# Three 16-head attentions rebuilt on transposed scores in PSUM

## The chip, the cores and the metric

One core of a Trainium2 chip runs the whole network as one launch. The metric is device microseconds of that launch, the median of several runs; lower is better. TensorE (PE), VectorE (DVE), ScalarE (ACT), GpSimd (POOL) and the DMA queue of SyncE (SP) run side by side and meet only at semaphores.

## What is computed

The reference is four layers of gated cross-attention and feed-forward over x of shape 128 x 64 x 128 (8192 tokens, float32), with a context of the same shape:

```python
x = x + tanh(g_xattn[l]) * attention_l(layernorm(x), ctx, ctx)
x = x + tanh(g_ffn[l])   * ffn_l(layernorm(x))
```

Layer 0 has heads of 64 columns and a routed expert feed-forward. Layers 1, 2 and 3 have 16 heads of 8 columns each; these three attentions are what is changed. For each batch of 64 tokens and each head:

```python
score = q_h @ k_h.T / sqrt(8)            # 64 x 64
# layer 1: softmax   layer 2: score where mask else -1e9, then softmax
# layer 3: s = where(score >= 0, score + 1, 1 / (1 - score)); s / sum(s)
out   = p @ v_h
```

Layer 1's feed-forward is a quantised one (bitlinear), those of layers 2 and 3 are routed to 8 experts, top-2 and top-1.

## The kernel before, in words

`build` (L2312) calls the stages one after another, with a barrier of all engines between them. `attention_narrow` (L522) is called three times: "l1" (softmax, with a head), "l2" (masked, with a tail), "l3" (stable, with both). Head (L176) fetches each token's expert row by indirect DMAs on POOL and adds it to x before the attention. Tail (L233) normalises the new x, multiplies it with the router's weights, picks experts and scatters rows to `slots` by indirect DMAs.

Each attention is a software pipeline over 32 items of 256 tokens (4 batches of 64). All engines have the same order written out by hand: `step(t)` emits the piece of each item that is due in beat t, and `t.live(s)` is true where item t-s exists. So a beat holds scores of one item, transposes of the one before, outputs of the one before that, and a semaphore count orders each piece against the others.

In a beat PE makes the scores of an item (L873, 16 matmuls that each use 32 rows and 64 columns of the array), projects q and k (L892, L893), transposes the probabilities 16 times through the two banks PT (L903), projects the values (L925), multiplies them with the transposed probabilities (L979, 32 matmuls with 18 columns moving: two heads at once), and projects out (L938, or L957 in the masked kind). An fp32 matmul appears as two instructions in the trace, a transpose and a bf16 matmul as one.

The keys are masked: k_t holds four copies of the projected k, copy j with all but the 8 rows of head j of each group of 32 rows set to zero (L814, four ACT instructions from PSUM). A matmul over 32 rows then gives four heads side by side in its 256 columns.

DVE takes the row maximum of the 128 x 2048 scores from PSUM (L739), subtracts it into the SBUF tile `prob` (L742), and in the masked kind first applies the mask (L730). ACT takes the exponential in SBUF (L843). ACT then copies every transposed block out of PT (L822). In the stable kind ACT makes relu(-s) (L800), log and exp of it (L835, L838), DVE makes max(s, 0) (L721) and adds the two (L781). DVE divides by the sums, which come out of L979 as two extra columns (L703, L707).

The tail's router multiplies on POOL (L358, two of 128 x 1024 a beat; the last items on DVE, L459) and DVE sums up (L464). Choices and slots of 4 items are made in one beat by a chain of small DVE instructions (L471 to L489, L436 to L451). L328 scatters.

Of the kernel before, what the change touches and what calls it, by code (L numbers as in the profile page):

```python
# [6 lines left out]
P = 128  # L7
# [32 lines left out]
C_COLS = C_ITEM + TOP2_TILES  # L40


def constants():

    c = np.zeros((P, C_COLS), np.float32)
    c[:, C_IDENT:C_IDENT + P] = np.eye(P)
    c[:, C_TRI:C_TRI + P] = np.triu(np.ones((P, P)))
    c[:, C_ONES:C_ONES + P] = 1.0
    for j in range(4):
        c[:, C_JMASK + j] = (np.arange(P) % 32) // 8 == j  # L50
    c[:, C_ECOL:C_ECOL + EXPERTS] = np.arange(EXPERTS)
    c[:, C_BLK:C_BLK + 16] = np.arange(16) * SLOTS
    c[:, C_ITEM:] = np.arange(TOP2_TILES)
    return c
# [121 lines left out]
class Head:  # L176
# [5 lines left out]
    def __init__(self, ph, g, rows, ks, own):  # L182
        self.g, self.rows, self.ks, self.own = g, rows, ks, own
        self.index = ph.sb("index", [P, 2, ks, 2], U32)
        self.got = ph.sb("got", [P, 2, ks, 2, D])
        self.term = ph.sb("term", [P, ks + own, 2, D])
        self.arrived = [ph.sem(f"arrived{k}") for k in range(2)]
        self.index_done, self.terms_done, self.combined = ph.sems("index_done terms_done combined")
        self.partly = [ph.sem(f"partly{k}") for k in range(ks + own - 1)]

    def gather(self, nc, pool, t, s, ready, count):

        g, n0, n2 = self.g, t.done(s), t.done(s + 2)
        pool.wait_ge(ready, count)
        for k in range(self.ks):
            last = nc.gpsimd.tensor_copy(self.index[:, t.par(s), k, :], g.get[k][:, bass.ds(t.item(s) * 2, 2)])  # L196
        last.then_inc(self.index_done, 1)
        for k in range(self.ks):
            for tile in range(2):
                pool.wait_ge(ready, count)  # L200
                wait(pool, self.index_done, n0)
                wait(pool, self.terms_done, n2)
                pool.indirect_dma_start(self.got[:, t.par(s), k, tile, :], None, self.rows,  # L203
                                        bass.IndirectOffsetOnAxis(ap=self.index[:, t.par(s), k, tile:tile + 1], axis=0),
                                        bounds_check=self.rows.shape[0] - 1, oob_is_err=False).then_inc(self.arrived[t.par(s)], 16)

    def combine(self, nc, pool, t, s, ready, count):

        g, n1, n2 = self.g, t.done(s), t.done(s + 1)
        landed = t.landed(s, 2 * self.ks)  # L210
        tiles = bass.ds(t.item(s) * 2, 2)
        xs = g.x[:, tiles, :]
        pool.wait_ge(ready, count)
        wait(pool, self.arrived[t.par(s)], landed)

        wait(pool, self.combined, n2)
        for k in range(self.ks):
            last = nc.gpsimd.tensor_tensor(self.term[:, k, :, :], self.got[:, t.par(s), k, :, :],
                                           g.weight[k][:, tiles].unsqueeze(2).broadcast_to([P, 2, D]), ALU.mult)
        if self.own:  # L220
            last = nc.gpsimd.tensor_tensor(self.term[:, 1, :, :], g.xn[:, tiles, :],
                                           g.weight[1][:, tiles].unsqueeze(2).broadcast_to([P, 2, D]), ALU.mult)
        last.then_inc(self.terms_done, 1)
        pool.wait_ge(ready, count)
        wait(pool, self.terms_done, n1)
        nc.gpsimd.tensor_tensor(self.term[:, 0, :, :], self.term[:, 0, :, :], self.term[:, 1, :, :],
                                ALU.add).then_inc(self.partly[0], 1)
        pool.wait_ge(ready, count)
        wait(pool, self.partly[0], n1)
        nc.gpsimd.tensor_tensor(xs, xs, self.term[:, 0, :, :], ALU.add).then_inc(self.combined, 1)  # L230


class Tail:  # L233

    def __init__(self, ph, g, w, bias, kind, slots, tiles):
        self.g, self.w, self.bias, self.kind, self.slots, self.tiles = g, w, bias, kind, slots, tiles
        self.ks = 2 if kind == "top2" else 1
        self.nb = BATCH_TILES // tiles
        wide, narrow = [P, BATCH_TILES, EXPERTS], [P, BATCH_TILES]
        self.w_s, self.bias_s = ph.sb("router_w", [P, EXPERTS, D]), ph.sb("router_b", [P, EXPERTS])
        self.st, self.mv = ph.sb("tail_st", [P, 2, tiles, 6]), ph.sb("tail_mv", [P, 2, tiles, 2])
        self.var_eps, self.rstd = ph.sb("tail_var_eps", [P, 2, tiles]), ph.sb("tail_rstd", [P, 2, tiles])  # L250
        self.prod = ph.sb("products", [P, tiles, EXPERTS, D])
# [9 lines left out]
        self.put = ph.sb("put", [P, 2, self.ks, tiles], U32)  # L261
        self.rows = ph.sb("rows_out", [P, 2, tiles, D])
        (self.w_in, self.part, self.stats, self.eps, self.rstd_done, self.xn_done, self.multiplied, self.summed,
         self.chosen_done, self.counted, self.counts_read, self.put_done, self.rows_copied, self.chained, self.totalled) = ph.sems(
            "router_w_in tail_part tail_stats tail_eps tail_rstd_done tail_xn_done multiplied summed "
            "chosen_done counted counts_read put_done rows_copied chained totalled")
        self.sent = [ph.sem(f"sent{k}") for k in range(2)]
        self.slots_clear = None
        self.loads = 16 * (1 + (bias is not None))

        self.ph, self.steps = ph, {}

    def load(self, sp):
        sp.dma_start(self.w_s[:, :, :], self.w.partition_broadcast(P)).then_inc(self.w_in, 16)
# [18 lines left out]
    def on_dve(self, t, s):  # L293

        return t.i is None and t.item(s) >= t.items - 7

    def depth(self):

        return 5 + self.nb + 3
# [2110 lines left out]
```

## Time and profile before

| what | us |
|---|---|
| median of 3 runs | 3622.13 (3612.05 to 3623.86) |
| the profiled execution, its own time | 3616.34 |
| its span, from first to last instruction | 3614.6 |
| busy: PE / DVE / ACT / POOL | 2554.5 / 2132.0 / 1498.5 / 1596.1 |

Busy shares are 71%, 59%, 41% and 44% of the span. No single engine is busy throughout: the stages have different limits, so the profile must be read stage by stage. The page's chain of waits covers only the last piece of the run. In the rows further down, "x" counts instructions, "PEclk" is the granted TensorE clock as a part of 2.4 GHz, and an arrow names what ended an idle time.

### The profile page before, as it was taken

How to read it: one execution, taken by the hardware profiler on the slowest of the kernel's cores; microseconds unless marked ns; L12 is line 12 of the kernel's file. 1: busy time of each engine (PE TensorE's matmuls, PEld its weight loads, DVE VectorE, ACT ScalarE, POOL GpSimd, SP SyncE). 2: the span in 40 equal slices, each digit the busy share in tenths (PEclk: the TensorE clock that was granted, in tenths of full speed). 3: DMA queues.
4: the chain of work that ended last, by engine and by line, in shares of the span. 5: the costliest groups of instructions: out<-in, count | busy, mean ns of one | idle time of the engine just before them, and what ended most of it. 6: DMA issues, size and time to landing. Idle time of an engine off the chain costs nothing. (4 is left out here: it accounts for less than half of the span.)

```text
span 3614.6 us, 84054 instructions
## 1 busy us (share of the span) xinstructions
PE 2554.5 (71%) x30961; PEld 1981.4 (55%) x30971; DVE 2132.0 (59%) x4394; ACT 1498.5 (41%) x2492; POOL 1596.1 (44%) x2184
## 2 busy tenths in 40 slices
PE   5999999977678886233687766609956877665490
PEld 4878778764557775122465555506634665554260
DVE  3767777661166664676578788854424666677312
ACT  3555555532255553677343333202215665553120
POOL 1333433440164430775024666440017788884207
PEclk9999999988888887555688778659976766675795
DMA  4000000003300000000000000015531000000243
GB/s 143 17 18 22 23 21 21 20 8 112 99 26 22 22 19 13 1 1 1 26 10 12 23 22 23 20 61 153 161 106 32 23 25 27 27 23 13 79 128 93
DMA packets 192979, 153.50 MB, mean 42 GB/s; under 512 B 24426, under 2 KB 170461, under 8 KB 192582
## 3 DMA queue, kind: packets, MB, share of 16 engines
q1 hardware_dynamic: 176198, 116.45, 11.0%
q0 software_dynamic: 16384, 31.69, 2.9%
q8 instruction: 257, 4.21, 0.5%
q14 instruction: 140, 1.15, 0.1%
HBM read 97.54 MB, written 52.43 MB: 41 GB/s over the span
## 5 line engine op out<-in xcount | busy, mean ns | idle before, releaser
L979 PE MATMUL l_B<-l_val,l_prob_t 128*64 128x18 f32 x6144 | 348.6, 220 | 44.1 <-ACT l_prob_t L822 36.9
L979 PEld LDWEIGHTS l_B<-l_val,l_prob_t 128*64 128x64 f32 x6144 | 340.4, 149 | 59.3 <-issue 59.3
L903 PE MATMUL l_PT<-const_table,l_prob 128*128 128x128 f32 x1536 | 267.9, 332 | 38.0 <-ACT l_prob_t L822 28.6
L1971 PE MATMUL experts_H<-experts_xs_t,experts_w 128*128 128x512 f32 x576 | 272.1, 616 | 10.1 <-ACT experts_hid L1951 4.9
L903 PEld LDWEIGHTS l_PT<-const_table,l_prob 128*128 128x128 f32 x1536 | 237.3, 178 | 68.8 <-issue 58.0
L822 ACT COPY l_prob_t<-l_PT 128x512 f32<-128x512 f32 x384 | 209.6, 601 | 132.8 <-PE l_PT L903 132.7
L203 POOL DMA_INDIRECT l_got<-rows,l_index x192 | 220.2, 1147 | 94.7 <-POOL l_index L196 50.3
L358 POOL TENSOR_TENSOR l_products<-l_router_w,xn_all 128x1024 f32<-128x1024 f32 x100 | 236.3, 2390 | 32.3 <-DVE logits L464 32.0
L883 PE MATMUL l_A<-const_table,l_xn 128*128 128x128 f32 x192 | 59.6, 410 | 251.7 <-issue 139.1
L328 POOL DMA_INDIRECT slots<-xn_all,put x192 | 202.0, 1052 | 60.6 <-issue 49.5
L632 POOL TENSOR_TENSOR l_var_eps<-l_mv,eps 128x2 f32<-128x2 f32 x96 | 26.4, 275 | 430.4 <-DVE l_mv L775 430.3
L196 POOL COPY l_index<-get 128x2 uint32<-128x2 uint32 x96 | 15.4, 177 | 435.2 <-DVE l_recip L659 435.2
L1372 POOL TENSOR_TENSOR l_var_eps<-l_mv,eps 128x1 f32<-128x1 f32 x64 | 12.1, 189 | 438.4 <-DVE l_mv L1454 438.4
L1990 PE MATMUL experts_Y<-experts_w,experts_hid 128*128 128x128 f32 x1664 | 198.8, 276 | 4.1 <-DVE experts_hid L1931 2.2
L1990 PEld LDWEIGHTS experts_Y<-experts_w,experts_hid 128*128 128x128 f32 x1664 | 192.6, 193 | 6.0 <-issue 6.0
L883 PEld LDWEIGHTS l_A<-const_table,l_xn 128*128 128x128 f32 x192 | 25.9, 190 | 308.1 <-issue 308.1
L807 ACT COPY l_xn_t<-l_A 128x256 f32<-128x256 f32 x96 | 35.6, 370 | 371.9 <-PE l_A L883 371.9
L814 ACT ACTIVATE l_k_t<-l_B,l_bk_masked,const_table 128x256 f32<-128x256 f32 x384 | 184.9, 568 | 0.0
L1411 DVE TENSOR_REDUCE l_top<-l_S 128x16 f32<-128x1024 f32 x64 | 78.3, 1224 | 172.0 <-PE l_S L1561 172.0
L1971 PEld LDWEIGHTS experts_H<-experts_xs_t,experts_w 128*128 128x128 f32 x576 | 104.5, 197 | 126.9 <-issue 126.9
L843 ACT ACTIVATE l_prob<-l_prob 128x2048 f32<-128x2048 f32 x64 | 122.9, 1921 | 117.9 <-DVE l_prob L742 117.9
L1907 DVE COPY experts_xs_t<-experts_X 128x512 f32<-128x512 f32 x72 | 49.8, 692 | 205.0 <-PE experts_X L1979 205.0
(309 smaller groups left out, 6835.8 us busy)
## 6 DMA issues: line engine op xcount, KB each, us to landing
experts_w<-in_F_w SPq DMA_DIRECT2D x104, 256.0 KB, 2.9
experts_xs<-slots SPq DMA_DIRECT2D x72, 256.0 KB, 2.8
rows<-experts_y SPq DMA_DIRECT2D x72, 256.0 KB, 2.9
l_ctx_t<-in_ctx_t SPq DMA_DIRECT2D x96, 128.0 KB, 2.1
slots<-l_zeros SPq DMA_DIRECT2D x64, 96.0 KB
experts_w<-in_F_w SPq DMA_DIRECT2D x40, 128.0 KB, 2.5
slots<-l_zeros SPq DMA_DIRECT2D x8, 512.0 KB, 5.5
l_ctx_t<-in_ctx_t SPq DMA_DIRECT2D x64, 64.0 KB, 2.0
```

What stands on the lines that cost most here:

```text
L203: pool.indirect_dma_start(self.got[:, t.par(s), k, tile, :], None, self.rows, bass.IndirectOffsetOnAxis(ap=self.index[:, t.par(s), k, tile ...
L328: pool.indirect_dma_start(self.slots, bass.IndirectOffsetOnAxis(ap=g.put[c][:, tile:tile + 1], axis=0), g.xn[:, tile, :], None, bounds_che ...
L358: last = nc.gpsimd.tensor_tensor(self.prod[:, tile, :, :], self.w_s[:, :, :], g.xn[:, bass.ds(t.item(s + 2) * k + tile, 1), :].broadcast_t ...
L814: last = nc.scalar.activation(k_t[:, t.par(3), j, :], B[:, 256:512], ACT.Identity, bias=bk_masked[:, j:j + 1], scale=g.const[:, C_JMASK + ...
L822: nc.scalar.copy(prob_t[:, 4 * c:4 * c + 4, :], PT[:, c % 2, :].rearrange("p (a q) -> p a q", a=4)).then_inc(pt_drained[c], 1)
L843: nc.scalar.activation(flat, flat, ACT.Exp).then_inc(prob_ready, 1)
L883: last = nc.tensor.transpose(A[:, P * tile:P * tile + P], xn[:, t.par(2), tile, :], ident)
L903: last = nc.tensor.transpose(PT[:, c % 2, P * a:P * a + P], prob[:, t.par(5), c, a // 2, 2 * (a % 2):2 * (a % 2) + 2, :].rearrange("p j k ...
L979: last = nc.tensor.matmul(B[64 * b:64 * b + 64, col:col + 18], prob_t[:, 4 * (hp // 2) + 2 * tile + hp % 2, 64 * b:64 * b + 64], val[:, t. ...
L1411: nc.vector.tensor_reduce(top[:, :, :], S[:, :, :, :], AX.X, ALU.max).then_inc(top_done, 1)
L1971: nc.tensor.matmul(H[:, c, :], w1_s[:, t.par(2), c, :], xs_t[:, t.par(2), :], start=True, stop=True).then_inc(h_filled[c], 1)
L1990: last = nc.tensor.matmul(Y[:, P * k:P * k + P], hid[:, t.par(3), c, P * k:P * k + P], w2_s[:, t.par(3), c, :], start=c == 0, stop=c == FC ...
```

## The change

`attention_narrow` becomes `attention_split` for all three layers, and `Tail` and `Router` (the class that layer 0 used) become one `Router`.

- Scores are computed twice in the softmax and masked kinds. SCORE fills the four banks X with the scores (queries in partitions); DVE reduces the maximum from them and they are dropped. The maximum is split into three bf16 parts, transposed by one matmul (TOP), spread with a mask of its own on DVE (top_d), and in the next beat PROB fills the four banks Z with "minus maximum" (16 bf16 matmuls) plus the transposed scores (keys in partitions). ACT takes exp straight from Z. The stable kind has no maximum and makes only the transposed scores.
- With keys in partitions the probabilities need no transposes. OUT multiplies them with the values in 64 matmuls of 64 rows x 64 columns, 9 columns moving, that go round the four quarters of the array. In the stable kind the two terms are not added: each is a matmul of its own, 128 in all, the two of a pair in the same quarter one behind the other.
- ACT writes q, four masked copies of q, k and four masked copies of k (ten instructions from PSUM; five in the stable kind).
- The mask is added by bf16 matmuls with the identity: 8 of 256 columns into X and 8 into Z.
- ACT copies the values; the bias of values and of the output projection is a bf16 matmul over 3 rows.
- The router's scores are PE work: two transposes, an ACT copy, two matmuls. Indices and rows of the indirect DMAs are read in place instead of copied first on POOL.
- Banks are shared: X by SCORE, TOP, output projection, router; Z by PROB, q/k (bank 0), values (bank 1), OUT (banks 2 and 3). The stable kind has q/k in X.

PE's order in a beat, cut to its core:

```diff
+                if t.live(PROB):
+                    wait(pe, qk_drained, t.done(PROB))
+                    if stable:
+                        wait(pe, plus_done, 4 * t.done(PROB + 1))
+                    else:
+                        wait(pe, diag_done, t.done(PROB))
+                        wait(pe, qk_drained, t.done(PROJ + 1))
+                    wait(pe, xv_drained, beats(t.t - 1, TURN, XV_BEATS))
+                    wait(pe, o_drained, t.done(OUT + 1))
...
+                                    nc.tensor.matmul(Z[64 * b:64 * b + 64, r, 256 * tile:256 * tile + 256], minus_ones[rows, :],
+                                                     top_d[rows, t.par(PROB), 4 * tile:4 * tile + 4, 64 * b:64 * b + 64],
...
+                                last = nc.tensor.matmul(Z[64 * b:64 * b + 64, r, 256 * tile:256 * tile + 256], k_t[rows, slot, seq],
+                                                        q_m[rows, slot, :, seq], start=stable and tile == 0, stop=tile == 1 and not folded)
...
+                    last.then_inc(p_filled, 1)
+                if t.live(SCORE) and not stable:
...
+                    last.then_inc(s_filled, 1)
+                if t.live(PROJ):
...
+                    if not stable:
+                        bank_read(t, 0)
...
+                if stable:
+                    stream_out(t)
+                if t.live(TURN) or t.live(PROB):
...
+                    bank_read(t, 1)
...
+                if t.live(OUT):
+                    wait(pe, prob_done, t.done(OUT) if stable else 4 * t.done(OUT))
+                    if stable:
+                        wait(pe, plus_done, 4 * t.done(OUT))
...
+                    bank_read(t, 2)
+                    bank_read(t, 3)
...
+                    for h in range(16):
+                        for tile in range(2):
+                            for b in range(2):
+                                rows, side = slice(64 * b, 64 * b + 64), 64 * (b ^ tile)
+                                for k, term in enumerate(terms):
...
+                if not stable:
+                    stream_out(t)
+                if t.live(SCORE) and not stable:
+                    wait(pe, split_done, t.done(SCORE))
+                    nc.tensor.matmul(TOP, split[:, :, :, :].rearrange("p r s a -> p (r s a)"), g.const_bf[:, C_IDENT:C_IDENT + P],
...
+                if turns(t):
...
+                if ranks(t):
```

ACT's order in a beat: the four exponentials (or relus), the q and k copies, the copies of xn and values, then the copy of the turned blocks (`wait(act, turned_filled, ...)`), and in the stable kind log and exp last. DVE's: maximum and its three parts, reciprocal and division of OUT, top_d, add to x, normalise, statistics, router. POOL's: rstd, combine, gather, scatter. In the masked kind POOL first makes one of the two expanded masks:

```diff
+                nc.gpsimd.tensor_scalar(hide[:, 1, :, :], mask_raw[:, 1, :, :], HIDE, -HIDE, ALU.mult, ALU.add).then_inc(hidden, 1)
```

## Rows read from the trace of the kernel before

**Rows 1.** Busy time by stage: layer 0, and the stretches of l1, l2, l3

```profile
core 0: us, PE busy (x) PEld busy (x) DVE busy (x) ACT busy (x) POOL busy (x), PEclk, DMA share, GB/s
0.00:968.60 968.60, 856.71 (x14344) 693.18 (x14344) 565.09 (x1300) 439.06 (x707) 300.18 (x452) 0.97 0.16 46
968.60:1427.60 459.00, 366.52 (x4544) 296.26 (x4544) 253.06 (x455) 219.33 (x385) 185.33 (x288) 0.81 0.08 21
...
1725.50:2411.50 686.00, 439.78 (x5001) 343.45 (x5001) 515.70 (x965) 213.53 (x353) 332.87 (x306) 0.75 0.06 22
...
2680.30:3383.30 703.00, 439.53 (x4616) 346.53 (x4616) 429.35 (x844) 340.82 (x449) 519.51 (x562) 0.64 0.09 26
```

**Rows 2.** Instructions on the scores tile: ns min/median/max, start of first and last

```profile
L730 DVE TENSOR_TENSOR l_prob<-l_S,l_limit x64: 1214/1216/1226, 1751.2 to 2305.0; 128x1024 f32<-128x1024 f32 x64
L739 DVE TENSOR_REDUCE l_top<-l_S x32: 2260/2292/2294, 1007.9 to 1394.4; 128x32 f32<-128x2048 f32 x32
L800 ACT ACTIVATE l_soft<-l_S x32: 1877/1877/1878, 2731.8 to 3292.1; 128x2048 f32<-128x2048 f32 x32
```

**Rows 3.** Waits in 1100:1300, 1900:2290, 2850:3250: us in total, times, longest

```profile
DVE l_recip L703 <- PE l_B L979: 53.5, 15, 4.2
...
ACT l_prob L843 <- DVE l_prob L742: 84.3, 20, 5.1
...
ACT l_soft L800 <- DVE l_prob L781: 110.2, 21, 9.4
```

**Rows 4.** Groups by line over the whole run: busy us, mean ns of one

```profile
L903 PE MATMUL l_PT<-const_table,l_prob 128*128 128x128 f32 x1536 | 267.9, 332 | 38.0 <-ACT l_prob_t L822 28.6 <-issue 8.3 <-DVE l_prob L781 0.6
...
L358 POOL TENSOR_TENSOR l_products<-l_router_w,xn_all 128x1024 f32<-128x1024 f32 x100 | 236.3, 2390 | 32.3 <-DVE logits L464 32.0
...
L822 ACT COPY l_prob_t<-l_PT 128x512 f32<-128x512 f32 x384 | 209.6, 601 | 132.8 <-PE l_PT L903 132.7
...
L814 ACT ACTIVATE l_k_t<-l_B,l_bk_masked,const_table 128x256 f32<-128x256 f32 x384 | 184.9, 568 | 0.0
...
L742 DVE TENSOR_TENSOR l_prob<-l_prob,l_top 128x2048 f32<-128x2048 f32 x32 | 90.9, 2841 | 3.3
```

**Rows 5.** Timeline, PE's bursts: start us, length us, instructions

```profile
401.50 1.16 PE L1576 MATMUL l_O<-l_prob_t,l_val 64*64 64x64 f32 x64
...
1203.68 0.67 PE L892 MATMUL l_B<-l_xn_t,l_wq 128*128 128x256 f32 x2
...
1207.98 0.71 PE L938 MATMUL l_B<-l_wo,l_ctx_out_t 128*128 128x128 f32 x4
...
1702.17 1.01 PE L2291 MATMUL bit_HT<-const_bf,bit_hq 128*128 128x128 bf16 x8 [3.77 <-DVE bit_hq L2195]
...
1749.07 2.02 PE L873 MATMUL l_S<-l_k_t,l_q_t 32*64 32x256 f32 x32 [2.54 <-ACT l_k_t L814]
...
2004.80 1.12 PE L873 MATMUL l_S<-l_k_t,l_q_t 32*64 32x256 f32 x32
...
2016.73 1.09 PE L957 MATMUL l_A<-l_wo,l_ctx_out 128*64 128x128 f32 x8
...
2019.19 2.92 PE L979 MATMUL l_B<-l_val,l_prob_t 128*64 128x18 f32 x58
```

**Rows 6.** Timeline, small steps of DVE and POOL and the end of l2

```profile
1202.37 0.36 DVE L703 RECIPROCAL l_recip<-l_B 128x32 f32<-128x32 f32 x1 [3.32 <-PE l_B L979]
...
1202.83 0.49 DVE L707 TENSOR_TENSOR l_ctx_out<-l_B,l_recip 128x128 f32<-128x128 f32 x2
...
2345.30 0.26 DVE L471 TENSOR_REDUCE l_of_batch<-l_chosen 128x8 f32<-128x64 bf16 x1
...
2349.44 0.23 DVE L489 TENSOR_TENSOR l_chosen<-l_hot 128x64 bf16<-128x64 f32 x1
...
2405.23 0.97 POOL L328 DMA_INDIRECT slots<-xn_all,put  x1 [0.30 <-issue]
2406.51 0.97 POOL L328 DMA_INDIRECT slots<-xn_all,put  x1 [0.30 <-issue]
```

More of the change, by code:

```diff
@@ L210, in combine @@
-        landed = t.landed(s, 2 * self.ks)
-        tiles = bass.ds(t.item(s) * 2, 2)
+        g, par, n = self.g, t.par(s), t.done(s)
+        tiles = slice(t.item(s) * 2, t.item(s) * 2 + 2)
         xs = g.x[:, tiles, :]
+        others = (self.got[:, par, 0, :, :], g.xn[:, tiles, :] if self.own else self.got[:, par, 1, :, :])
         pool.wait_ge(ready, count)
[L214 to L219, printed above, removed]
@@ L400, in dve, with transpose @@
-    def dve(self, nc, dve, t, s, updated):
+        return nc.tensor.matmul(bank[:, 0:n], ones, self.before[:, :].unsqueeze(1).broadcast_to([P, BATCH_TILES, EXPERTS]),
+                         start=False, stop=True)
+    def transpose(self, nc, pe, t, s, out):
+        wait(pe, self.xn_done, t.done(s + 2))
+        for tile in range(self.tiles):
+            last = nc.tensor.transpose(out[:, P * tile:P * tile + P], self.g.xn[:, t.item(s + 2) * self.tiles + tile, :], self.g.const[:, C_IDENT:C_IDENT + P])
+        return last
@@ new lines, in score, with read_transposed, read_scores @@
+    def score(self, nc, pe, t, s, out):
+        for tile in range(self.tiles):
+            last = nc.tensor.matmul(out[:, EXPERTS * tile:EXPERTS * tile + EXPERTS], self.xn_t[:, t.par(s + 3), tile, :], self.w_s[:, :],
+                                    start=True, stop=True)
+        return last
+    def read_transposed(self, nc, t, s, bank):
+        return nc.vector.tensor_copy(self.xn_t[:, t.par(s + 2), :, :], bank[:, 0:P * self.tiles].rearrange("p (k n) -> p k n", n=P))
+    def read_scores(self, nc, t, s, bank):
+        k = self.tiles
+        return nc.vector.tensor_copy(self.g.logits[:, bass.ds(t.item(s + 3) * k, k), :],
+                                     bank[:, 0:EXPERTS * k].rearrange("p (k e) -> p k e", e=EXPERTS))
@@ L519, in chain, with beats, attention_split @@
         return link
-def attention_narrow(nc, g, name, gate_col, wq, bq, wk, bk, wv, bv, wo, bo, kind, mask=None, head=None, tail=None):
-    ITEMS, TPI = TILES // 2, 2
+def beats(t, first, n):
+    return max(0, min(t - first + 1, n))
+def attention_split(nc, g, name, gate_col, wq, bq, wk, bk, wv, bv, wo, bo, kind, mask=None, head=None, router=None):
+    ITEMS = TILES // 2
     SCALE = float(1.0 / np.sqrt(np.float32(8)))
-    folded = kind == "masked"
+    HIDE = float(2.0 ** 100)
+    folded, stable = kind == "masked", kind == "stable"
+    STAT, NORM, TURN, PROJ = 1, 2, 3, 4
+    SCORE, PROB, OUT, STREAM = 5, 6, 7, 8
+    SLOTS_QK, SLOTS_CTX = 4, 8
+    LAST = STREAM + 1
     with ExitStack() as ctx:
@@ L578, in _, with turns, ranks, reused @@
+        TURNED_BEATS = (ITEMS + (T0 + 2 if tail else OUT)) - TURNED_FROM
+        RANKS_BEATS = ITEMS + 1
+        def turns(t):
+            return (not folded and t.live(OUT)) or (tail and t.live(T0 + 2))
+        def ranks(t):
+            return tail and (t.live(T0 + 3) or tail.batch(t, T0 + 4))
+        def reused(t, s, slots):
+            return 16 * ((t.t - s) // slots + 1) if t.t >= s else 0
         @block.sync
@@ new lines, in step @@
+                    if folded:
+                        pe.wait_ge(hidden, 2)
+                        for tile in range(2):
+                            for r in range(4):
+                                last = nc.tensor.matmul(Z[:, r, 256 * tile:256 * tile + 256], g.const_bf[:, C_IDENT:C_IDENT + P],
+                                                        hide[:, 1, 2 * t.item(PROB) + tile, :].unsqueeze(1).broadcast_to([P, 4, 64]),
+                                                        start=False, stop=tile == 1)
```

1063 lines of the change are left out of this document (395 added, 668 removed).

## The prediction

> **What bounds the kernel now.** I cut the run into stages first, since only three of them change. l1, l2 and l3 take 459, 686 and 703 us, 1848 of 3614.6; the rest stays [rows 1]. Then I took the beat of each: 31 steps between the first and the last score instruction give (1394.4 - 1007.9)/31 = 12.5 us for l1, (2303.9 - 1751.2)/31 = 17.8 for l2 (the last L730 is the second of its beat, 1.1 us in), (3292.1 - 2731.8)/31 = 18.1 for l3 [rows 2]. The remainder of a stage is its start and end. Last, the waits of the steady middle tell who is late. In l1 DVE waits for PE's output matmuls in every beat and PE is busy 80% of the stage: PE bounds it. In l2 ACT waits for DVE's subtraction and DVE has 515.7 busy us of 686: DVE bounds it. In l3 ACT waits for DVE's add up to 9.4 us, while POOL is busy 519.5 of 703: a ring over DVE, PE and ACT with POOL close behind [rows 1, 3].
>
> **What goes.** Of PE: 16 transposes a beat, 1536 in all, 332 ns each with overlap, 267.9 us busy. Of ACT: their four copies at 601 ns. Of DVE: the subtraction (2.3 to 2.8 us a beat in l1 and l2), the two masks at 1.2 us (l2), the add (l3), and the router's sum (l2, l3). Of POOL: the router's products, 2.39 us twice a beat [rows 2, 4].
>
> **What comes, priced at full clock, one beat.** Sixteen score matmuls are 1.1 us, against 2.0 at the low clock, and a q/k projection is 2 x 0.6 us [rows 5]. The 16 "minus maximum" matmuls stream as many columns in one bf16 pass, not four: 0.3 us. Eight mask matmuls: the 128-column bf16 ones took 1.01/8 = 126 ns each in a stage at the low clock, so 256 columns at twice the clock are again 126 ns, 1.0 us for eight. Transposes of xn, value bias and values: 0.4 + 0.1 + 0.7 = 1.2. Output projection: 8 instructions in 1.1 us plus bias is 1.2, twice that in l2 [rows 5]. A bank of 512 columns read by ACT is about 0.6 us, a masked copy of 256 columns just under 0.5 in a run of four (568 ns with overlap) [rows 4]. The maximum stays 2.3 us; its three parts are four dependent small DVE steps at 0.3 (15 such steps run from 2345.30 to 2349.67) [rows 2, 6]; top_d reads PSUM like L730, 1.2 us [rows 2].
>
> The unknown is OUT: 128 instructions (l1, l2) or 256 (l3) on quarters of the array. No row has this shape. The nearest below is L1576, also 64 x 64 and going round the quarters: 64 in 1.16 us, 18 ns each. The nearest above is L979, which stays in one half for 16 instructions: 58 in 2.92 us, 50 ns [rows 5]. I take 18, since shape and rotation are L1576's: 2.3 us, and 4.6 in l3.
>
> **l1.** The ring is PE and DVE: PROB 1.4, SCORE to 2.5, q/k to 3.7, values to 4.9 (ACT's exponentials end at 1.4 + 0.2 + 2.1 = 3.7 and hold up nothing), OUT to 7.2, projection to 8.4, TOP to 8.5, top_d with its two handovers to 10.0, and the next PROB waits for that. ACT beside it: 3.7 + 10 copies (4.8) + two copies (0.8) = 9.3, so the masked copies are covered by 0.7 us, no more. PE idles 1.5 us of 10. Before it was idle about as little and got a clock of 0.81 [rows 1]. I add 0.5: **10.5**. Gain 31 x 2.0 = 61.
>
> **l2.** With the masks PROB is 2.4 and SCORE ends at 4.5; q/k 5.7, values 6.9, OUT 9.2, projection 11.6, TOP and top_d 13.1. DVE has about 11.1 of work in a plain beat: 2.3 + 1.2 + 0.9 [rows 6] + 1.2, and some 5.5 for stream, two normalisations with statistics, and a quarter of the choices and slots. The choices (4.4 us in one beat of four) make DVE late for the next maximum by some 4 us, of which PE's own work hides 2: 0.7 us a beat. With the clock **14.5**. Gain 31 x 3.3 = 103.
>
> **l3.** ACT holds the ring: from the first relu, four relus and DVE's last maximum 3.1, OUT to 7.7, division and handovers (0.36 + 0.49 + 0.2) to 8.8, four transposes to 9.7, ACT's copies to 10.6, log and exp (2.0 + 1.9) to 14.6, because the next relu stands behind them. The q and k copies lie under OUT. POOL is under it: 519.5/32 = 16.2 busy us a beat now, less 4.8 for the products, is 11.5 [rows 1, 4]. PE has a hole of some 3 us while it waits for the next relus, so part of OUT runs at the low clock as in the stage before (0.64): + 2, **16.5**. Gain 31 x 1.6 = 49.
>
> **Starts and ends.** Each start has a chain of seven small DVE steps for the biases, +2 to +3. In l2 POOL expands 4096 mask bytes before its first root. DVE's mask pass before was 2.3 us; POOL's products run at 2.39 us per 1024, four times that is 9.6 [rows 4]. I take 8, near POOL's own row, and 2 for the second mask load. From the last L730 to the end of l2 it was 2411.5 - 2305.0 = 106 [rows 1, 2]. Without the router's products on DVE I count 41 until the last item is normalised, then POOL's 36 scatters at 1.28 apart [rows 6], 46, and 4 to the next stage: 91, 15 less. l3 has half the scatters, 18 or 23, but its last choices and slots are late by 4: 91 becomes 33 + 27 + 11 = 71, 20 less. Sum: l1 +3, l2 -3, l3 -17. Layer 0 loses a POOL copy that nothing waits for; its POOL is busy 300 of 969 us [rows 1]: 0. ctx loads run 8 slots ahead instead of 2; PE waited for none before: 0.
>
> **Sum.** -61 - 103 - 49 + 3 - 3 - 17 = -230. From the profiled time of 3616.3 that is 3386; this execution lay 6 below the median, so **3390**.
>
> **A rule that speaks against it.** L979 stays on all 128 rows and costs 50 ns an instruction, L1576 changes its rows at every matmul and costs 18 [rows 5]. The Trainium skill, "TensorE: Matmul & The Clock Gate", Part 3, says that a weight load overlaps running matmuls only when its row group differs. By that rule the pairs of l3, two matmuls on the same 64 rows, would lose part of the overlap, and the sum is that of the first rival; the trace agrees with it in both rows, though neither has pairs.
>
> **Rivals.**
> - *l3's pairs don't overlap.* Half of the 256 instructions at 50 ns and half at 18 is 8.7 us, 4.1 over the forecast, all on l3's ring: beat 20.6, 31 x 4.1 = 127, **3517**. For: pairs are adjacent. Against: PE may run ahead across quarters. Chance 0.17.
> - *The clock stays low in the new holes.* If l3 runs at the low clock throughout, OUT doubles (+4.6) and transposes (+0.8): 20 instead of 16.5, +108; if l1 and l2 get 0.7 instead of about 0.9, +1.5 each a beat, +93. One of the two gives about **3490**. For: l3 had 0.64. Against: PE's load rises in l1 and l2. Chance 0.15.
> - *Slower.* The quarters don't overlap at all. Then OUT costs 50 ns for 512 instructions over the three layers, 32 x 0.512 x 31 = 508 us more, **3898**. Each ns per instruction costs 15.9 us, so the loss begins at 18 + 230/15.9 = 32 ns. What decides it is whether PE works on quarters side by side when each matmul streams 9 columns only and the weight loads are all there is. For: L979. Against: L1576 with the same weight loads. A milder form at 36 ns gives 3676. Chance 0.08.
> - *It doesn't do what it says.* The "DMAs between buffers on chip" are in neither kernel here, so that part of the title is worth 0; the rest is in the code. Inside the forecast.
>
> **Numbers.** Forecast 0.60, rivals 0.17, 0.15, 0.08. Low end: full clock everywhere and late choices hidden, 0.5, 1.0 and 1.9 us a beat less, -105 and rounding for a quicker OUT: 3280. High end: the first rival: 3520. Faster 0.91, within 0.3% (some 11 us, about what a measurement of this kernel can tell from no change) 0.02, slower 0.07.
>
> **What would show it.** Score instructions of l1, l2, l3 10.5, 14.5 and 16.5 us apart; OUT as bursts of 2.3 and 4.6 us; PE waiting for top_d at most 1.5 us a beat in l1; ACT never idle between OUT's copies and the next relu in l3; POOL's mask pass of 8 us at the start of l2; the clock of l1 and l2 at 0.85 or more. The forecast is wrong if OUT costs over 25 ns an instruction, if ACT's ten copies end later than top_d, or if l3's beat is over 18.

## The result, and the profile after

The changed kernel takes **3364.9 us** (median of 4 runs, 3360.4 to 3368.2) where the kernel before takes 3618.3 beside it: a ratio of 0.930, 95% interval 0.928 to 0.932. The profiled execution spans 3358.6 us against 3614.6, so 256 us went. The kernel before takes the same in every session below (3617 to 3626); the changed one does not, and run again unchanged in one later session it took 3656.

By stage (the new kernel's windows: us, then busy time of PE, PEld, DVE, ACT, POOL with instructions, the granted clock, DMA share, GB/s; the first three are l1, l2 and l3, the others their steady middles):

```profile
967.00:1358.00 391.00, 308.36 (x7392) 223.40 (x7392) 219.74 (x527) 237.86 (x545) 179.82 (x256) 0.76 0.09 25
1655.30:2198.00 542.70, 413.23 (x8392) 319.32 (x8393) 299.44 (x958) 240.33 (x545) 185.90 (x257) 0.84 0.09 28
2464.90:3126.70 661.80, 489.54 (x10184) 391.64 (x10184) 225.01 (x835) 295.30 (x481) 335.45 (x448) 0.57 0.10 27
1010.00:1330.00 320.00, 277.25 (x6836) 202.32 (x6844) 199.14 (x466) 221.88 (x509) 154.04 (x220) 0.81 0.09 24
1690.00:2090.00 400.00, 359.19 (x7560) 276.36 (x7560) 249.58 (x765) 224.20 (x508) 118.15 (x180) 0.93 0.07 22
2520.00:3020.00 500.00, 422.07 (x8900) 336.21 (x8900) 185.16 (x662) 259.46 (x421) 266.62 (x364) 0.59 0.10 28
```

Against [rows 1], l1 lost 68 us, l2 143 and l3 41; the rest of the kernel lost 4. DVE fell from 515.7 to 299.4 us in l2 and POOL from 519.5 to 335.5 in l3, as the removals say. The beats, as one instruction's 32 places in l1, l2 and l3:

```profile
L717 DVE TENSOR_TENSOR l_top_d<-l_X,const_table x32: 1212/1224/1225, 1009.3 to 1336.7; 128x1024 bf16<-128x1024 f32 x32
L717 DVE TENSOR_TENSOR l_top_d<-l_X,const_table x32: 1216/1225/1226, 1693.4 to 2108.0; 128x1024 bf16<-128x1024 f32 x32
L701 DVE RECIPROCAL l_recip<-l_Z x32: 356/358/358, 2544.3 to 3080.0; 128x32 f32<-128x32 f32 x32
```

(1336.7 - 1009.3)/31 = 10.6, (2108.0 - 1693.4)/31 = 13.4, (3080.0 - 2544.3)/31 = 17.3 us. Forecast were 10.5, 14.5 and 16.5.

**l1.** One seam between two beats (start, duration, engine, idle time before it and who ended it):

```profile
1103.90 0.49 DVE L709 TENSOR_TENSOR l_ctx_out<-l_Z,l_recip 128x128 f32<-128x128 f32 x2
1104.40 1.22 DVE L717 TENSOR_TENSOR l_top_d<-l_X,const_table 128x1024 bf16<-128x1024 f32 x1
1104.82 0.45 ACT L797 COPY l_val<-l_Z 128x256 f32<-128x256 f32 x1
1105.83 0.83 PE L852 MATMUL l_Z<-l_top_d,l_minus_ones 32*64 32x256 bf16 x16 [0.88 <-DVE l_top_d L717]
```

TensorE waits for top_d, which ends at 1105.62; ScalarE's tenth masked copy and its values copy are done at 1105.27, only 0.35 us earlier. The steps are the forecast's.

**l2.** TensorE's order in a plain beat, which wraps round from 1880.62 of the next one:

```profile
1873.59 0.71 PE L920 MATMUL l_Z<-l_wv,l_ctx_t 128*128 128x128 f32 x4
1874.23 2.21 PE L940 MATMUL l_Z<-l_val,l_prob_t 64*64 64x9 f32 x128
1876.37 0.29 PE L989 MATMUL l_X<-l_bias_rows,const_bf 3*64 3x256 bf16 x1
1878.86 0.23 PE L950 MATMUL l_X<-const_bf,l_split 128*128 128x128 bf16 x1
1880.62 0.42 PE L852 MATMUL l_Z<-l_top_d,l_minus_ones 32*64 32x256 bf16 x16 [0.95 <-issue]
1880.83 1.07 PE L860 MATMUL l_Z<-l_q_m,l_k_t 32*64 32x256 f32 x32
1881.84 1.05 PE L866 MATMUL l_Z<-l_hide,const_bf 128*128 128x256 bf16 x8
1882.72 1.04 PE L884 MATMUL l_X<-l_hide,const_bf 128*128 128x256 bf16 x8
1883.69 1.12 PE L892 MATMUL l_X<-l_k_m,l_q_t 32*64 32x256 f32 x32
```

The prices stand: masks 1.0 us for eight, scores 1.1, OUT 2.2 (17 ns an instruction). Neighbours overlap by 0.1 to 0.2 us at each seam, so a plain beat is 12.5 us and not 13.1. The clock was 0.93 in the steady middle: 1.00 in the plain beats, 0.75 to 0.88 in those of 13.9 us and more.

**l3.** From one division to the next relus, and the next OUT's end:

```profile
2750.31 0.36 DVE L701 RECIPROCAL l_recip<-l_Z 128x32 f32<-128x32 f32 x1 [6.97 <-PE l_Z L940]
2751.39 0.66 PE L960 MATMUL l_X<-const_table,l_ctx_out 128*128 128x128 f32 x2 [1.19 <-DVE l_ctx_out L709]
2752.57 0.37 ACT L804 COPY l_ctx_out_t<-l_X 128x256 f32<-128x256 f32 x1 [7.62 <-PE l_X L348]
2753.10 2.02 ACT L812 ACTIVATE l_soft<-l_soft,const_table 128x2048 f32<-128x2048 f32 x1
2755.21 1.91 ACT L815 ACTIVATE l_soft<-l_soft 128x2048 f32<-128x2048 f32 x1
2757.03 2.04 ACT L772 ACTIVATE l_soft<-l_Z 128x512 f32<-128x512 f32 x4
2757.69 2.49 DVE L695 TENSOR_SCALAR l_prob_t<-l_Z 128x512 f32<-128x512 f32 x4 [1.16 <-issue]
2767.45 0.36 DVE L701 RECIPROCAL l_recip<-l_Z 128x32 f32<-128x32 f32 x1 [7.27 <-PE l_Z L940]
```

ScalarE goes from the copies through log and exp to the relus without a gap, as forecast, and idles 7.6 us beside OUT. OUT runs from 2760.4 to 2767.3, 6.9 us for 256 instructions, nearly all of it at the low clock (0.56 in this burst, 0.50 in most).

**Start of l2.** POOL's mask pass took 3.6 us, not 8:

```profile
1665.63 3.64 POOL L597 TENSOR_SCALAR l_hide<-l_mask_raw 128x4096 bf16<-128x4096 uint8 x1 [19.15 <-DMA l_mask_raw<-in_mask]
1665.71 3.56 DVE L634 SCALAR_TENSOR_TENSOR l_bq_masked<-const_table,l_bq 128x4 f32<-128x4 f32 x1
1674.59 0.48 DVE L734 BATCH_NORM_STATS2 l_st<-x_stream 128x6 f32<-128x128 f32 x2
```

### The profile page after: what moved, and what is told of

The parts are those of the page before. It is cut to its first block and busy times, and to the rows that moved or that the text cites. A ratio compares the mean times of both kernels' runs of the same rounds, so it can differ in the third digit from the quotient of the medians.

```text
span 3358.6 us, 107440 instructions
## 1 busy us (share of the span) xinstructions
PE 2519.9 (75%) x42779; PEld 1927.9 (57%) x42779; DVE 1673.6 (50%) x4452; ACT 1498.1 (45%) x2876; POOL 1241.9 (37%) x1925
## 5 line engine op out<-in xcount | busy, mean ns | idle before, releaser
L200 POOL DMA_INDIRECT l_got<-rows,get x192 | 197.8, 1030 | 486.1 <-DVE l_bias_rows L651 436.8
L940 PE MATMUL l_Z<-l_val,l_prob_t 64*64 64x9 f32 x12288 | 352.1, 218 | 8.5 <-issue 6.0
L940 PEld LDWEIGHTS l_Z<-l_val,l_prob_t 64*64 64x64 f32 x12288 | 338.8, 160 | 23.4 <-issue 16.1
L940 PE MATMUL l_Z<-l_val,l_soft 64*64 64x9 f32 x4096 | 216.2, 247 | 2.7 <-issue 2.3
L774 ACT ACTIVATE l_prob_t<-l_Z 128x512 f32<-128x512 f32 x256 | 132.2, 602 | 189.4 <-PE l_Z L866 89.8
L674 DVE TENSOR_REDUCE l_top<-l_X 128x32 f32<-128x2048 f32 x64 | 146.6, 2290 | 133.3 <-PE l_X L892 133.3
L940 PEld LDWEIGHTS l_Z<-l_val,l_soft 64*64 64x64 f32 x4096 | 210.3, 214 | 3.7 <-issue 3.6
L860 PE MATMUL l_Z<-l_q_m,l_k_t 32*64 32x256 f32 x3072 | 160.9, 546 | 1.5 <-ACT l_val L797 0.9
L1685 ACT ACTIVATE experts_hid<-experts_H,experts_b_scaled 128x512 f32<-128x512 f32 x128 | 78.2, 689 | 158.5 <-DVE experts_b_scaled L1645 155.3
L1254 PE MATMUL l_R<-l_ctx_t,l_wk 128*128 128x128 f32 x1024 | 132.5, 283 | 0.0
```

The source lines that it names most:

```text
L674: V.tensor_reduce(top[:, :, :].rearrange("p r a -> p (r a)"), X[:, :, :].rearrange("p r (a k) -> p (r a) k", k=64), AX.X, ALU.max).then_in ...
L774: nc.scalar.activation(prob_t[:, t.par(PROB), r, :], Z[:, r, :], ACT.Exp).then_inc(prob_done, 1)
L860: last = nc.tensor.matmul(Z[64 * b:64 * b + 64, r, 256 * tile:256 * tile + 256], k_t[rows, slot, seq], q_m[rows, slot, :, seq], start=stab ...
L940: last = nc.tensor.matmul(Z[side:side + 64, 2 + b, 9 * h:9 * h + 9], term[rows, t.par(OUT), h // 4, col:col + 64], val[rows, t.par(OUT), t ...
L1254: last = nc.tensor.matmul(R[:, BANK[name], P * k:P * k + P], w[:, 4 * (c % 2) + k, :], moving, start=True, stop=True)
L1685: nc.scalar.activation(hid[:, t.par(2), c, :], H[:, c, :], ACT.Gelu if kind == "gelu" else ACT.Relu, bias=b1_scaled[:, t.par(2), c:c + 1], ...
```

## The experiments

After the first there were five sessions on four chips, called A to E here (D and E on one chip); the kernel before took 3621, 3618, 3621, 3626 and 3617 us in them. Times are medians, or the one time there is (experiments 2, 3, 4, 5 and 9). The changed kernel doesn't take the same in all sessions, so a comparison across two of them is named as one. The diffs are cut, and a comment in them stands for code in words.

**Session A. 1: ScalarE's log and exp before the turned copies.**

```diff
+    if t.live(PROB) and stable:      # log and exp, moved up
+        ...
     if turns(t):
         act.wait_ge(ready, 1)
         ...
-    if t.live(PROB) and stable:
-        ...
```

> The new kernel with ScalarE's log and exp of the third attention issued before the copies of the turned output instead of behind them; nothing else is changed. Theory: ScalarE holds l3's ring, as predicted, and its 2.0 + 1.9 us stand in it while ScalarE idles 7.9 us beside OUT. Then the beat of 17.3 us loses 4.1 and goes to 13.2, unless TensorE at the low clock (some 15.3 us of work a beat) comes first: between 13.2 and 15.3, 62 to 127 us less, 3240 to 3303. Rival 1, TensorE is already the bound of l3 at its low clock: at most the hole of 1.2 us before the transposes goes, beat about 16.5, 3340. Rival 2, GpSimd bounds (11.5 us): it would show at a beat below 13 only.

**2 and 3: the order of OUT.** Loops were h, tile, b. Now:

```diff
-for h in range(16):
-    for tile in range(2):
-        for b in range(2):
+for b in range(2):                   # 2: same rows, output side alternates
+    for h in range(16):
+        for tile in range(2):
...
+for b in range(2):                   # 3: same quarter
+    for tile in range(2):
+        for h in range(16):
```

> OUT's loops are turned so that 32 instructions in a row (64 in l3) have their weights in the same 64 rows, alternating only the half of the output partitions; same instructions, same sums. Theory, the row group decides what overlaps: an instruction costs 50 ns as L979 did and not 17, OUT takes 6.4 us in l1 and l2 (+4.2 a beat, all on PE's path) and 12.8 in l3 (+5.9): 32 x 14.3 = 458 us more, 3820. Rival, the side of the output is enough to keep two loads going, or the weight load alone is the price: OUT stays at 2.2 and 6.9 us, 3365.

> As the run before, but each quarter of the array does its 16 (32 in l3) instructions in a row, so neither rows nor output side alternate. If the row group decides, the time is that of the run before (3820 if 50 ns an instruction). If a change of the output side was what saved the run before, this one alone is slow: 3820 against 3365. If nothing of the order matters, both are 3365.

**4: pairs apart in l3.**

```diff
 for h in range(16):
+    for k, term in enumerate(terms):
         for tile in range(2):
             for b in range(2):
-                for k, term in enumerate(terms):
```

> In l3 the two instructions of a pair (same 64 rows, same output) are no longer adjacent: the order goes round the four quarters with the positive part, then round them with the other. l1 and l2 are unchanged. Theory: pairs cost nothing, and OUT takes 6.9 us in l3 for the low clock alone (27 ns an instruction at a granted clock of 0.56): OUT stays within 0.3 us of 6.9 and the time within 10 us of 3365. Rival, the first rival of the prediction in a smaller size: adjacent pairs lose their overlap and are what lifts 4.6 to 6.9; then OUT falls by up to 2.3 us, 32 x 2.3 = 74, to 3291.

Measured: 3623.5 us (ratio 1.000, 0.999 to 1.002), 3950.7, 4588.7 and 3652.2. The first and the last made no sense: 258 and 287 us more for edits that touch l3 alone. The beats of l1 had grown too, to 13 us, and OUT's line showed why ("who waited for it" of OUT, in us and times; the new kernel's first run, then experiment 1):

```profile
  DVE l_recip L701: 304.0, 88
```

```profile
  DVE l_recip L701: 528.2, 90
```

VectorE waits 224 us longer for OUT's end, most of the 258. TensorE stands still inside OUT for nothing that the profile shows, which it calls "issue": 28.0 us in 65 waits in the first run and 292.6 in 665 here. That count takes in the matmuls and their weight loads side by side, so it tells of the same stall twice; on the matmuls alone it is 8.3 and 128.5 us, and short stalls are not in it. It serves as a marker, not as a sum. Where no such waits fall, the order's effect is plain. One burst of OUT in l1, for the new kernel, experiment 2 and experiment 3, and the two halves of the last one (us, busy time of PE and PEld with instructions, clock, DMA share, GB/s):

```profile
1111.79 2.21 PE L940 MATMUL l_Z<-l_val,l_prob_t 64*64 64x9 f32 x128
```

```profile
1431.61 3.70 PE L940 MATMUL l_Z<-l_val,l_prob_t 64*64 64x9 f32 x128
```

```profile
1103.41 8.95 PE L940 MATMUL l_Z<-l_val,l_prob_t 64*64 64x9 f32 x128
```

```profile
1103.41:1107.90 4.49, 4.49 (x84) 4.49 (x85) 1.00 0.21 58
1108.00:1112.30 4.30, 4.30 (x46) 4.27 (x44) 0.50 0.01 4
```

The first two bursts are at full clock. The third is so only in its first half, where an instruction takes 54 ns (4.49 us for 84); the whole burst's 70 ns is a mean over both clocks. So at full clock it is 17 ns an instruction when it goes round four quarters, 29 when the rows stay and the output side alternates, 54 when one quarter does all: about 1 to 2 to 4, once the last matmul's own time is taken off (15, 28, 54). Both theories for 2 missed: 29 lies between 17 and 50. Experiment 3 has the 50 ns that its first theory named, but took 4589 us and not 3820, since much of it ran at the low clock. One thing was not separated: OUT writes each of the two row halves to a PSUM bank of its own, so experiment 2 stops the alternation of rows and of banks together; the step from 2 to 3 changes the output side alone.

Experiment 4's OUT takes 6.8 us in the last beats of l3, where no such waits fall, as the new kernel's does.

**Session B. Control.** Nothing is edited.

> The new kernel again, unchanged, as a control. In the four runs before this one TensorE stalls inside OUT in l1 too, where the first and the last of them leave its instructions as they are: in gaps of about 0.65 us after every eighth instruction, 'issue' idle time of 293 us before the OUT instructions against 28 in the first run of the new kernel. The gaps stop at the beat at which the context loads run out (l1 and l3, beat 25 of 32), so they hang on transfers that run beside OUT. Theory, the supply of TensorE's instructions varies with the placement of a run, not with the edits: the control too takes up to 260 us more than 3365. Rival, the edits (ScalarE's order, the order of OUT) cause it in some way: the control is at 3365 within 10, and its OUT takes 1.8 us in l1 and 6.8 in l3.

Measured: 3364.6 us, ratio 0.930 (0.926 to 0.934), "issue" 25.0 us in 53 waits. That is the number the rival named. The edits were still possible as the cause, so the control went along with them.

**Session C. Control, experiment 1 again, and 5: top_d early.**

```diff
-V.tensor_tensor(top_d[...], ...).then_inc(diag_done, 1)
+for half in range(2):
+    V.tensor_tensor(top_d[:, ..., 4*half:4*half+4, :], ...).then_inc(diag_done, 1)
...
+# PE: per tile, wait for that half, then 'minus maximum', then scores
...
+# l2: TOP between the two halves (b) of the output projection
```

> The new kernel unchanged, a second control, on the same chip as the two runs after it. Theory 1, the supply of TensorE's instructions hangs on the chip: OUT takes the same in all runs of one chip, either 1.8 us in l1 in all of them or over 3 us in all. Theory 2, it hangs on the program: the control has 1.8 us and 3365 again wherever it runs.

> ScalarE's log and exp before the copies of the turned output, the same kernel as in the first run, beside the control on its chip. Theory 1 (the chip decides): with an undisturbed supply it gives what was expected then, a beat of 13.2 to 15.3 in l3 and 3240 to 3303 in all; if the control is slow on this chip too, it is slow by the same 258. Theory 2 (the program decides): 3620 again, with OUT at 3.5 us in l1, although TensorE's instructions are the same, one by one, as in the control.

> Two parts in l1 and l2. In both, top_d is made in two halves and TensorE starts on the first ('minus maximum' and scores of the first tile) while VectorE makes the second. In l2 alone the turning of the maximum (TOP) stands in the middle of the output projection and not behind it. Theory, TensorE's wait for top_d sets l1's beat: its hole of 0.9 us shrinks by 0.6, and the clock falls less: l1's beat 10.56 goes to 9.5 to 9.9, 20 to 33 us less. In l2 a hole of some 0.9 us goes too and the late maximum of the choices is hidden: 13.4 to 12.2 to 12.8, 19 to 37 less. Together 3295 to 3325 where the control is at 3365. Rival, ScalarE's masked copies, only 0.35 us earlier than top_d, come last as soon as top_d is early: l1 gains at most 0.35 x 31 = 11 us.

Measured: control 3655.6 (ratio 1.008, 1.006 to 1.011), experiment 1 3617.4 (0.998, 0.996 to 1.000), experiment 5 3638.5. The unchanged kernel is 290 us slower here than in B, and by 0.8% slower than the kernel before. So it is the place or the time of the run, and not the program; the kernel before doesn't show it. Beside this control experiment 1 gains 38 us and experiment 5 (one run) 17. In the beats that no stall falls on, the edits show what they are worth: experiment 1's last beats of l3 take 15.5 against 17.3, experiment 5's early beats of l2 mostly 11.0 to 11.7 against 12.5, its late ones of l1 10.2 against 10.3. What stands beside the waits? One burst of OUT in l1 of this control in its four pieces, with GpSimd's issues, and then the issues beside the first run's burst:

```profile
1119.82 1.09 POOL L200 DMA_INDIRECT l_got<-rows,get  x1 [0.16 <-issue]
1119.93 0.87 PE L940 MATMUL l_Z<-l_val,l_prob_t 64*64 64x9 f32 x44
1121.09 0.32 PE L940 MATMUL l_Z<-l_val,l_prob_t 64*64 64x9 f32 x5 [0.30 <-issue]
1121.21 1.00 POOL L200 DMA_INDIRECT l_got<-rows,get  x1 [0.31 <-issue]
1121.86 0.24 PE L940 MATMUL l_Z<-l_val,l_prob_t 64*64 64x9 f32 x2 [0.45 <-issue]
1122.60 1.36 PE L940 MATMUL l_Z<-l_val,l_prob_t 64*64 64x9 f32 x77 [0.50 <-issue]
```

```profile
1111.54 1.09 POOL L200 DMA_INDIRECT l_got<-rows,get  x1 [0.16 <-issue]
1112.93 1.00 POOL L200 DMA_INDIRECT l_got<-rows,get  x1 [0.30 <-issue]
```

While GpSimd issues a gather, TensorE gets its instructions a few at a time, 0.7 to 0.8 us apart, and when the gathers are through, 77 come in one go. In the first run the same gathers lie beside the burst of 2.21 us above, without a stall. Over the three layers an OUT instruction of this control took 58 to 72 ns while GpSimd was issuing and 24 to 29 otherwise, by where one draws the borders of an issue (the next expectation's 3859 in 241 us is 62 and not 58); in the first run it took 21 to 22 in both. In l1 the stalls end at beat 25, where the gathers do; in l2 they begin after eleven beats, with the scatters. The loads of the context are not the cause: in l2 they run from the first beat on, and the first eleven bursts take 1.8 to 2.3 us as in the first run. OUT's bursts together are 571 us long here and 347 in the first run, 224 of the 291 us; the rest lies outside OUT. The profile has a second sign of such a session. VectorE and ScalarE have waits in it that it puts down to no instruction of this core, "remote"; this control's longest group, and one of experiment 6 of the next session (us, times, longest):

```profile
DVE l_top L674 <- remote: 32.5, 5, 7.7
```

```profile
ACT l_soft L775 <- remote: 37.9, 17, 2.7
```

Every run of sessions A and C has such waits, and neither the first run nor the one of B has any.

**Session D. 6: GpSimd's gathers and scatters wait for OUT, and 7: all early issues.**

```diff
+if t.live(OUT):
+    pool.wait_ge(ready, 1)
+    wait(pool, o_filled, t.done(OUT))
 if head and t.live(0):
     head.gather(nc, pool, t, 0, ready, 1)
```

Experiment 7 is 1 and 5 together, and in l3 the router's product goes ahead of the turned transposes:

```diff
+if stable:
+    rank(t)                          # the block 'if ranks(t)', as a function
 if turns(t):
     ...
-if ranks(t):
-    ...
+if not stable:
+    rank(t)
```

> The new kernel with one wait more: GpSimd issues the gathers and scatters of a beat only when OUT of that beat has ended (before it issued them when its own queue came to them, in part beside OUT). Reason: in the runs at 3617 to 3656, an OUT instruction took 58 ns (3859 of them in 241 us) while GpSimd was issuing an indirect DMA and 25 to 27 ns otherwise, against 20 to 25 in both cases in the runs at 3365. Theory, the issue of indirect DMAs keeps TensorE's instructions away on some chips: on such a chip OUT in l1 falls from 3.5 to 1.8 us and in l2 from 6 to 7 to about 2, and the time comes to 3370 to 3420; on a chip of the other kind it stays at 3365, or 5 to 20 more for gathers that land later. Rival, the context loads or plain bad luck of the chip do it: on a chip of the first kind it stays at 3655.

> All early issues together: top_d in halves and TOP inside l2's output projection (the third run of the last call), ScalarE's log and exp before the turned copies (l3), and in l3 the router's product and counts before the turned transposes, where TensorE waits for the division. In the undisturbed beats of the last call the first gave 11.0 to 11.7 in l2 against 12.5, and the second 15.5 in l3 against 17.3. Theory: on a chip that does not starve TensorE, l1 10.4, l2 12.2 with the choices, l3 14.6 to 15.3, so 5 + 37 + 62 to 84 less than 3365: 3240 to 3265. On a chip that does: the gains outside the starved bursts only, 3580 to 3600. Rival, the low clock in l3 gives nothing back since TensorE is busy throughout: l3 stays above 16.5 and the time above 3300 on the first kind of chip.

Measured: 3437.9 us (ratio 0.949, 0.946 to 0.952) and 3557.7 (0.982, 0.978 to 0.985). Experiment 7 shows that the session starves TensorE (OUT 3.7 to 4.7 us in most beats of l1). The wait cures OUT: it is 1.8 us from first to last instruction in most beats of l1 and l2, 6.8 in l3, "issue" 20.9 us. The new kernel without the wait was not run in D. Beside experiment 7, which has all the early issues and no wait, experiment 6 is 120 us faster; against the control of session C it is 218, across two sessions. The wait moves the issues and the transfers that follow them together, so which of the two holds TensorE up is not shown. Its time is above the 3370 to 3420 expected, and experiment 7's below its 3580 to 3600. What remains against 3365 is in l2 (beat 13.8) and the beats 12 to 24 of l3, 20.8 us each, where four gathers and two scatters stand in a row and ScalarE then starts late:

```profile
2867.70 1.91 ACT L818 ACTIVATE l_soft<-l_soft 128x2048 f32<-128x2048 f32 x1
2872.25 1.09 ACT L775 ACTIVATE l_soft<-l_Z 128x512 f32<-128x512 f32 x2 [2.64 <-remote]
```

Its inputs were there (the scores ended at 2867.6); GpSimd's last scatter ended at 2871.2. That ScalarE is starved in the same way fits, but was not tested; experiment 9 below, with the same order of GpSimd's issues in session E, has no such wait.

**Session E. 8: 6 and 7 together, and 9: 6 with idle matmuls.** Experiment 9's matmuls stand in two holes of TensorE in l3, and their output is overwritten unread:

```diff
+def fill(n):
+    for _ in range(n):
+        nc.tensor.matmul(Z[:, 0, 0:256], identity_bf, const_bf[:, 0:256], start=True, stop=True)
...
+fill(6)                              # between OUT and the turned transposes
...
+fill(4)                              # before the transposes of xn, once bank 0 is read
```

> The early issues of the seventh experiment and GpSimd's wait of the sixth together, as a candidate for the best version. Measured before on chips that starve TensorE: the new kernel 3656, early issues alone 3558, the wait alone 3438. Theory, the two add up where they touch different things: l1 10.4 to 10.5, l2 14.2 less 1.2, l3 between 15.5 and 20.7: in its beats without scatters the log and exp give 1.8, in those with four gathers and two scatters in a row GpSimd's 7.7 us of issues keep ScalarE waiting (2.6 us) and give little back. 3438 - 37 - 20 to 50 = 3350 to 3380 on such a chip. On a chip that does not starve: 3250 to 3330. Rival, GpSimd's late issues are l3's ring altogether, and the early issues give nothing there: 3400.

> The sixth experiment's kernel with matmuls that no one reads in two holes of TensorE in l3: six of 256 columns (bf16) between OUT and the transposes that wait for the division, four between the output projection and the transposes of xn. They add no result. Theory, the low clock of l3 (two thirds and more of each beat at half speed) comes from these holes and costs 2.7 us a beat: with them filled the first eleven beats of l3 go from 17.3 towards 14.6, and OUT from 6.8 to under 6. Rival, the clock is set by something else (what ScalarE or the whole beat does, or holes elsewhere): OUT stays at 6.8, and the beat stays at 17.3 or is up to 0.5 longer for the added matmuls.

Measured: **3233.4 us, ratio 0.894 (0.892 to 0.896)** and 3343.2. Experiment 8 is 10.6% faster than the kernel before. The new kernel did not run in E; by the two ratios to the kernel before, 0.894 and 0.930, experiment 8 is 3.9% faster than it. Its three layers, and the steady middle of l3:

```profile
966.00:1345.00 379.00, 307.69 (x7392) 229.85 (x7392) 222.69 (x557) 237.73 (x545) 180.75 (x256) 0.77 0.10 25
1642.00:2160.00 518.00, 415.37 (x8392) 318.04 (x8392) 302.35 (x990) 240.42 (x545) 186.31 (x257) 0.84 0.10 30
2426.00:3000.00 574.00, 429.69 (x10184) 329.71 (x10184) 221.83 (x835) 298.95 (x481) 337.12 (x448) 0.67 0.11 32
2480.00:2940.00 460.00, 393.00 (x9657) 301.64 (x9658) 197.07 (x708) 284.26 (x452) 274.70 (x373) 0.71 0.11 31
```

From division to division the beats are 10.1, 12.3 and 14.5 us, against 10.4, 13.4 and 17.2 of the control in B. l1 gained 0.3 where 0.7 to 1.1 were expected of experiment 5: the rival, ScalarE's copies next in line by 0.35 us. l3's beats 12 to 24 are 14.7 here and 16.9 in experiment 9, not 20.8, with GpSimd's order that of session D. So session E didn't starve the engines: neither run of it has a "remote" wait, while both of D have. That is why 3233 lies under the 3250 to 3330 expected of such a session and not beside D's times. What experiment 8 takes in a session that starves was not measured, and neither was what the wait is worth in one that doesn't: experiment 9's beats of l1 and l2, 10.5 and 13.1 us from division to division with the wait, against 10.4 and 13.1 of the first run, say that it costs little there.

Experiment 9: l3's beat is 16.7 against 17.2, its first eleven 16.5 against 17.2 in the first run and 17.1 in experiment 6, which has the same wait and no filling. The clock of the middle of l3 was 0.69 against 0.59. Filled holes give a part of the clock back, 0.5 to 0.7 us a beat of the 2.7 that the theory charged to it, though ten matmuls were added. It is one run. Both theories had a part: the holes matter, and they are not all of it.

## Why the prediction was right, point by point

- **The sum.** Forecast 230 us less than the profiled 3616.3, measured 256. Beats: 61 forecast and 59 measured in l1, 103 and 138 in l2, 49 and 25 in l3. Starts and ends: +3 and -9, -3 and -5, -17 and -17. The errors of l2 and l3, 35 and -24, nearly cancel, and that the total is better than its parts is luck.
- **OUT, the unknown.** 18 ns was taken, from L1576, against 50 from L979 [rows 5]; it is 17. Experiments 2 and 3 show that with the shape kept the order alone takes it to 29 and 54, the last near the 50 of L979. The third rival had that price right and its 3898 was still too mild (experiment 3: 4589, with OUT's order alone changed), because it counted full clock: at the low one an instruction costs 102 ns so, and 27 in turn.
- **l1.** The ring's steps are as forecast; the cover over ScalarE was 0.35 us, not 0.7. The clock was 0.76 (0.81 in the middle), not the 0.85 that I gave as a sign. Two beats, from OUT to OUT, one wholly at full clock and a plain one:

```profile
1039.10:1048.00 8.90, 7.74 (x232) 6.01 (x231) 6.17 (x15) 7.17 (x18) 3.79 (x7) 1.00 0.14 34
1122.10:1132.40 10.30, 9.07 (x233) 6.57 (x231) 6.58 (x17) 7.39 (x18) 5.63 (x8) 0.83 0.12 29
```

  So "to 10.0" was 8.9 and the 0.5 for the clock was some 1.4. That they add up to 10.6 for 10.5 is luck.
- **l2: the terms that were mis-sized.** "TOP and top_d 13.1" is 12.5, in part for the overlap at the seams. 0.7 for the choices and 0.7 for the clock were 0.9 together: the plain beats are at full clock, and the long ones, where the choices are late, have the low clock in them too, so the two can't be told apart here. DVE's work in a plain beat was 7.8 us (7.76 busy in 12.5) and not 11.1, so the choices had more room than I counted. Together 13.4 for 14.5.
- **l3: the other one.** By the rows above, the first relu to OUT takes 3.4 us, OUT to the reciprocal 7.0, from there to ScalarE's copy 2.3, to the log 0.5, to the next relu 3.9. The forecast had 3.1, 4.6, 2.0, 0.9 and 4.0, and 2 for the clock in part of OUT; it should have been all of OUT, 2.4. The clock of 0.59 is one burst of full speed and then half speed in each beat. So the second rival, low clock throughout, was the truth in l3 in kind; its price, 20, was not: OUT came to 6.9, not 9.2. And one of my signs of being wrong did come true in l3: OUT at over 25 ns an instruction, 27. The 17 or 18 ns of a burst at full clock have the last matmul's own time in them; from first instruction to last it is 15 ns (1.85 us for 128 in l1), and 27 at the low one.
- **Pairs (first rival).** They cost nothing at the low clock: in the last beats of l3, which no gather disturbs, OUT takes 6.8 us in either order (experiment 4 and the control of C), and experiment 4 at 3652 lies beside the control at 3656, though in another session that starves. At full clock it was not tested. I had weighed the Trainium skill's rule that a weight load overlaps only when its row group differs ("TensorE: Matmul & The Clock Gate", Part 3). Experiment 2 keeps the rows and alternates output sides, and costs 29 ns, neither 17 nor 54: the output's side counts as well as the rows, against the page's "only".
- **Start of l2.** The mask pass was priced by POOL's two-input products, 2.3 ns an element; with one byte input it ran at 0.9. First statistics 19.3 us into the stage against 13.2, so 6 and not 12 more; it was partly set against an end that got 11 us shorter, not 15.
- **What no step and no rival had.** The supply of TensorE's instructions. The change makes them 1.6 to 2.2 times as many in these layers (7392 matmuls for 4544 in l1, 10184 for 4616 in l3), 128 or 256 short ones in a row. In session C this took 290 us back, more than the whole gain, and in D a kernel with one wait was 120 us ahead of one without it that had every other gain. The forecast of 3390 is right for the first session and for B; in C it would have been wrong by 7%, outside its range, with "faster" wrong too.

## What to carry to other kernels

Many tiny matmuls are cheap if neighbours go round the quarters of the array, and nearly four times as dear if one quarter does them all; so order the innermost loops by quarter before anything else. Where an engine issues instructions at tens of ns each, keep GpSimd's indirect transfers out of that stretch with a wait (it cost little where nothing starved, and was worth at least 120 us where something did), and time such a kernel, with its control, in more than one session. When one engine idles in a ring for 7 us a beat, look for work of the same engine that stands behind the ring's last step and needs nothing of it: ScalarE's log and exp were such work.

## What the runs showed of the hardware that I had not expected

- OUT instructions of 9 columns: 17, 29 and 54 ns with four, two and one quarter in turn at full clock; in l3 at the low clock 6.8, 13.2 and 26.0 us for 256, which is 27, 52 and 102 ns. All three orders take nearly twice as long at the low clock.
- The same program took 3365 us in two sessions and 3656 in a third, always the same within a session (3641 to 3660 over 8 runs). The difference lies in waits between small groups of TensorE's instructions while GpSimd issues indirect transfers. Why only some sessions have it was not found. It is not the chip alone: D and E share one, and D has it and E has not.
- A DVE instruction on 128 x 4 elements took 3.56 us while POOL's mask pass of 3.64 us ran beside it (the rows of the start of l2), in a kernel where small steps take 0.3.
- Idle matmuls in holes raised the clock of l3's middle from 0.59 to 0.69 and shortened l3 by some 14 us (31 x 0.45, one run, against a control of another session), although they add work.
- VectorE and ScalarE wait for something "remote" in all seven profiled kernels of A and C and in both of D (28 to 67 us in sum), and in none of the first session, B and E. So it is probably not TensorE's supply alone.
